# Row lengths of the Gram matrix added in PSUM, four wide comparisons, and edge sums per batch, in a hypergraph, attention and filter kernel

## What is computed

```
sq = sum(xf * xf, axis=-1)
d2 = sq[:, :, None] + sq[:, None, :] - 2.0 * einsum('bic,bjc->bij', xf, xf)
incidence = sqrt(maximum(d2, 0)) < 16.0
xe = einsum('bnc,dc->bnd', xf, W_fc) + b_fc
deg_e = sum(incidence, axis=1)
edge = einsum('bve,bvc->bec', incidence, xe) / deg_e
vert = einsum('bve,bec->bvc', incidence, edge) / deg_v
x = x + silu(batchnorm(vert + xf))
```

## Time and profile before

| | |
|---|---|
| median of 3 runs | 52.59 us |
| lowest and highest | 52.2 and 52.71 us |
| the profiled execution's own time | 52.18 us |
| its span, first to last instruction | 50.4 us |
| PE / DVE / ACT / POOL busy in it | 42.9 / 23.3 / 21.0 / 9.6 us |

### The profile page before, as it was taken

The page is one execution under the profiler, slowest core; times in us unless marked ns, Lnnn a source line. Parts: engine busy times, 40 slices in busy tenths (PEclk is TensorE's granted clock), DMA queues, the critical chain, the costliest instruction groups (busy, mean ns, idle before and its releaser), DMA issues.

```text
span 50.4 us, 1575 instructions
## 1 busy us (share of the span) xinstructions
PE 42.9 (85%) x658; PEld 25.5 (51%) x658; DVE 23.3 (46%) x81; ACT 21.0 (42%) x55; POOL 9.6 (19%) x36
## 2 busy tenths in 40 slices
PE   2999994999879999787999968648999999999910
PEld 1332743564436974436787424226455646548800
DVE  1057629999756460326648775745001400403420
ACT  0664999805222992499895882050003100000000
POOL 4760408880002275000000000430000000000000
PEclk9999999999999999999999999999999999999999
DMA  0599400000000000000000000000000000000011
GB/s 0 145 311 362 142 0 0 0 0 0 13 0 0 0 20 0 0 0 0 0 13 0 0 13 0 0 0 0 0 0 0 7 0 0 13 0 0 0 52 52
DMA packets 1303, 1.44 MB, mean 29 GB/s; under 512 B 272, under 2 KB 1040, under 8 KB 1296
## 3 DMA queue, kind: packets, MB, share of 16 engines
q1 hardware_dynamic: 1008, 1.26, 7.8%
q10 hardware_dynamic: 288, 0.08, 0.7%
HBM read 1.21 MB, written 0.13 MB: 27 GB/s over the span
## 4 chain that ended last, share of the span: by engine, by line
PE 57%; DVE 13%; ACT 9%; issue 7%; POOL 5%; DMA 4%; POOLq 0%; DVEq 0%
PE bank L536 22%; PE bank L362 8%; DMA x_sb<-in_x 4%; PE bank L579 4%; PE bank L350 3%; PE bank L370 3%; PE quad L527 3%; ACT L252 3%; PE bank L478 2%; PE quad L492 2%; PE bank L503 2%; DVE hgraph L647 2%; POOL h L202 1%; PE quad L469 1%; POOL tiny L205 1%
## 5 line engine op out<-in xcount | busy, mean ns | idle before, releaser
L536 PE MATMUL bank<-v,gh 128*128 128x512 f16 (+7 forms) x48 | 7.5, 317 | 0.0
L536 PEld LDWEIGHTS bank<-v,gh 128*128 128x128 f16 x48 | 4.2, 98 | 3.4 <-issue 0.2
L252 ACT ACT_TABLE_LOAD x4 | 5.1, 1283 | 1.7 <-PEq L852 1.6
L337 PE MATMUL bank<-busy 128*128 128x512 f16 x9 | 4.0, 629 | 0.9 <-DVE busy L613 0.9
L536 PE MATMUL bank<-v,gl 128*128 128x512 f16 (+7 forms) x24 | 3.8, 317 | 0.8 <-DVE v L775 0.8
L362 PE MATMUL bank<-phis,mst 32*32 32x64 f32 x256 | 4.2, 289 | 0.0
L788 DVE TENSOR_TENSOR yb<-bank,maskp 128x512 f32<-128x512 f32 x2 | 1.4, 690 | 5.9 <-PE bank L536 5.9
L362 PEld LDWEIGHTS bank<-phis,mst 32*32 32x32 f32 x256 | 3.7, 110 | 0.5 <-issue 0.5
L647 DVE TENSOR_SCALAR hgraph<-quad,thr 128x256 f16<-128x256 f32 x8 | 3.4, 471 | 0.4 <-PE quad L392 0.4
L337 PE MATMUL quad<-busy 128*128 128x512 f16 x10 | 3.3, 381 | 0.0
L536 PEld LDWEIGHTS bank<-v,gl 128*128 128x128 f16 x24 | 2.0, 98 | 2.4 <-issue 1.1
(11 more groups left out here) (171 smaller groups left out, 77.3 us busy)
## 6 DMA issues: line engine op xcount, KB each, us to landing
m_sb<-in_mfilt SPq DMA_DIRECT2D x1, 512.0 KB, 3.6
cst<-in_consts SPq DMA_DIRECT2D x1, 271.0 KB, 3.8
x_sb<-in_x SPq DMA_DIRECT2D x1, 128.0 KB, 2.1
phi_sb<-in_phi SPq DMA_DIRECT2D x1, 128.0 KB, 2.5
out<-res SPq DMA_DIRECT2D x2, 64.0 KB, 1.5
sml<-in_small ACTq DMA_DIRECT2D x1, 64.0 KB, 2.6
mu_sb<-in_mu SPq DMA_DIRECT2D x1, 64.0 KB, 3.5
sml<-in_small ACTq DMA_DIRECT2D x1, 12.0 KB, 2.3
```

The source lines that it names most:

```text
L252: act.activation(spare[:, len(loads) - 1:len(loads)], eps[:, 0:1], func)
L337: pe.matmul(dst, busy[:, 0:1].broadcast_to([P, P]), busy[:, 0:1].broadcast_to([P, 512]), start=True, stop=True)
L536: mm = pe.matmul(acc[:, :, lag:HT], g[:, s, :, :].rearrange("p e a -> p (e a)"), v2[:, part, :, begin + lag:begin + HT], start=(first and ...
```

## The change

The row term of the distance is now added in PSUM as well, by 16 further matmuls whose weights are `hq` and whose moving operand is -0.5 (`neghalf`, now 256 columns wide). The 4 matmuls with `maskhalf`, the tile itself with its POOL fills, and the thresholds `thr` on DVE are gone. The additions are ordered by part, all with the high part first, and PE waits for the low part only ahead of the second. With nothing left that differs from row to row, the comparison uses the constant -128 and takes a whole batch of 512 columns at once: four comparisons in place of eight. `edge_sums` waits for its batch's comparison; the two of batch 3 now stand together ahead of the matmul with `ones32`.

```diff
--- before.py
+++ after.py
@@ -79,8 +79,7 @@
         mu_sb = sb("mu_sb", [P, NX, C])
         mumix = sb("mumix", [P, NX, C])
         mtap = sb("mtap", [P, C])
-        neghalf = sb("neghalf", [P, P], F16)
-        maskhalf = sb("maskhalf", [P, B], F16)
+        neghalf = sb("neghalf", [P, T], F16)
         hq = sb("hq", [P, 2, T], F16)
         ones32 = sb("ones32", [P, P])
         busy = sb("busy", [P, 1], F16)
@@ -102,7 +101,6 @@
         st = sb("st", [P, 8])
         h = sb("h", [P, T])
         hsq = sb("hsq", [P, T])
-        thr = sb("thr", [P, 2, B])
         hb = sb("hb", [P, T])
         hgraph = sb("hgraph", [P, B, 2, T], F16)
         h2 = sb("h2", [P, 2, T], F16)
@@ -183,10 +181,6 @@
                 pool.wait_ge(sem("pool_step"), step[0])
 
             pool.memset(neghalf[:, :], -0.5).then_inc(sem("half"), 1)
-            link(pool.memset(maskhalf[:, :], 0.0))
-            for b in range(B):
-                pool.memset(maskhalf[32 * b:32 * b + 32, b:b + 1], -0.5).then_inc(sem("half"), 1)
-            pool.wait_ge(sem("half"), 1 + B)
             pool.memset(u2[:, :, 0:PAD], 0.0).then_inc(sem("zero"), 1)
             pool.memset(ones32[:, :], 1.0).then_inc(sem("ones"), 1)
             pool.iota(tpos[:, :], [[1, T]], base=0, channel_multiplier=0,
@@ -378,21 +372,24 @@
                 for n in range(2):
                     pe.matmul(quad[:, b, n * T:(n + 1) * T], h[r, n * HT:(n + 1) * HT], h[r, :],
                               start=(n == 0), stop=False, skip_group_check=True)
-            pe.wait_ge(sem("half"), 1 + B)
+
+            pe.wait_ge(sem("half"), 1)
             pe.wait_ge(sem("hsq_high"), 1)
-            pe.wait_ge(sem("hsq_low"), 1)
-            for n in range(2):
-                for part in range(2):
-                    mm = pe.matmul(gbank[0][:, n * B:(n + 1) * B], hq[:, part, n * HT:(n + 1) * HT],
-                                   maskhalf[:, :], start=(part == 0), stop=(part == 1))
-            mm.then_inc(sem("sqi_psum"), 1)
-            for b in range(B):
-                r = slice(32 * b, 32 * b + 32)
-                for part in range(2):
-                    mm = pe.matmul(quad[:, b, :], neghalf[r, :],
+            for part in range(2):
+                if part:
+                    pe.wait_ge(sem("hsq_low"), 1)
+                for n in range(2):
+                    for b in range(B):
+                        r = slice(32 * b, 32 * b + 32)
+                        pe.matmul(quad[:, b, n * T:(n + 1) * T], hq[r, part, n * HT:(n + 1) * HT], neghalf[r, :],
+                                  start=False, stop=False, skip_group_check=True)
+                for b in range(B):
+                    r = slice(32 * b, 32 * b + 32)
+                    mm = pe.matmul(quad[:, b, :], neghalf[r, 0:P],
                                    hq[r, part, :].unsqueeze(1).broadcast_to([32, 2, T]),
                                    start=False, stop=(part == 1), skip_group_check=True)
-                mm.then_inc(sem(f"gram{b}"), 1)
+                    if part:
+                        mm.then_inc(sem(f"gram{b}"), 1)
 
             pe.wait_ge(sem("ident16"), 1)
             pe.wait_ge(sem("h_high"), 1)
@@ -406,7 +403,7 @@
 
             def edge_sums(b, n):
 
-                pe.wait_ge(sem("compare"), 2 * b + n + 1)
+                pe.wait_ge(sem("compare"), b + 1)
                 acc = edgebank[0][:, :, b, :] if b < B - 1 else edgebank[1][:, :, 0, :]
                 for half in range(2):
                     pairs = hgraph[:, b, n, half * P:(half + 1) * P]
@@ -434,11 +431,11 @@
                     elif b or n:
                         fill()
             edge_sums(B - 1, 0)
+            edge_sums(B - 1, 1)
             pe.wait_ge(sem("ones"), 1)
             pe.wait_ge(sem("bp"), 1)
             pe.matmul(gbank[0][:, 2 * B:2 * B + 1], ones32[:, :], bp, start=True, stop=True)\
               .then_inc(sem("bound_psum"), 1)
-            edge_sums(B - 1, 1)
             fill()
             pe.wait_ge(sem("rdeg"), 2)
             turn_rows(gbank[1], rdeg[:, :, :].rearrange("p h b -> p (h b)"), "rdegc_psum")
@@ -637,15 +634,11 @@
             dve.wait_ge(sem("phi_in"), 16)
             dve.tensor_reduce(phimax, phi_sb[:, :], AX_X, ALU.max, apply_absolute_value=True)\
                .then_inc(sem("phimax"), 1)
-            dve.wait_ge(sem("sqi_psum"), 1)
-            dve.tensor_scalar(thr[:, :, :].rearrange("p h b -> p (h b)"), gbank[0][:, 0:2 * B], -1.0, -RADIUS2 / 2,
-                              ALU.mult, ALU.add).then_inc(sem("thr"), 1)
-
-            def compare(b, n):
+            def compare(b):
 
                 dve.wait_ge(sem(f"gram{b}"), 1)
-                dve.tensor_scalar(hgraph[:, b, n, :], quad[:, b, n * T:(n + 1) * T], thr[:, n, b:b + 1],
-                                  None, ALU.is_gt).then_inc(sem("compare"), 1)
+                dve.tensor_scalar(hgraph[:, b, :, :].rearrange("p n t -> p (n t)"), quad[:, b, :], -RADIUS2 / 2,
+                                  1.0, ALU.is_gt, ALU.mult).then_inc(sem("compare"), 1)
 
             def degrees(acc, first, last):
                 dve.wait_ge(sem("edge_psum"), last)
@@ -662,25 +655,20 @@
                 dve.tensor_tensor(edge2[:, 1, :, first:last, :], edge[:, :, first:last, :],
                                   edge2[:, 0, :, first:last, :], ALU.subtract).then_inc(sem("edge_low"), 1)
 
-            dve.wait_ge(sem("thr"), 1)
-            compare(0, 0)
-            compare(0, 1)
-            compare(1, 0)
-            compare(1, 1)
-            compare(2, 0)
+            compare(0)
+            compare(1)
+            compare(2)
             dve.wait_ge(sem("wts"), 1)
             dve.wait_ge(sem("sig"), 2)
             mark(dve.scalar_tensor_tensor(out=wsum[:, 0, :], in0=wts, scalar=sig, in1=sml[:, P_EXPERT:P_EXPERT + NX],
                                           op0=ALU.mult, op1=ALU.mult, accum_out=ws))
-            compare(2, 1)
+            compare(3)
             settle()
-            compare(3, 0)
             dve.wait_ge(sem("rowphi"), 1)
             dve.wait_ge(sem("mul1"), 1)
             dve.scalar_tensor_tensor(out=bp, in0=rowphi, scalar=ws, in1=mul1, op0=ALU.mult, op1=ALU.add)\
                .then_inc(sem("bp"), 1)
             degrees(edgebank[0], 0, B - 1)
-            compare(3, 1)
             mark(dve.tensor_scalar(wsp, ws, PTOP / 4, None, ALU.mult))
             dve.wait_ge(sem("rdeg"), 1)
             edges_scaled(edgebank[0], 0, B - 1)
```

## The result

The changed kernel takes 52.3 us (median of 22 runs, 51.79 to 52.52) against 52.64 us for the one before on the same chips (22 runs, 52.08 to 53.65): a ratio of 0.9947, 95% interval 0.9922 to 0.9972. That is 0.28 us faster, with 0.15 to 0.41 as the interval. The result lies within the 1% band of the forecast and inside its range, but the gain is four times the 0.07 us that was worked out. The profiled execution took 51.90 us with a span of 50.1.

A forecast was written before the change was run, and what follows sets the result against it. One dependent sequence was taken as the bound, through batch 3's scaled edges, with PE's queue the new limit. Gain 0.19 - s (s 0.12) = 0.07 us: profiled 52.18 to 52.11, median 52.5, range 52.1 to 52.95.

The forecast's parts named there:

- the 1% band of the forecast: Whole kernel: time within about 1% (0.53 us) of the kernel before, given a chance of 0.81.
- the 0.07 us that was worked out: Batch 3's edges: start at 11.53 + s against 11.72, a gain of 0.19 - s, or 0.07 us.
- The price of the row term on PE: PE's Gram stage: 0.28 us removed, four rounds of 0.10 added, so the turn of h comes 0.12 us later.
- The shift s = 0.12 of everything behind it: From PE's turn of h onward: turn and first comparison 0.12 us later; bounds zero and 0.52.
- PE as the new limit (11.53 + s): Batch 3's edges: PE's queue through hb and the edge sums sets their start, at 11.65; DVE waits.
- chain B: Not forecast, named after measuring: from wsum over the fourth comparison and bp into the ones32 matmul, toward batch 3's edges.
- P: Chain forecast to hold the end: PE's queue through ht, rowm, hb and the edge sums; batch 3's edges at 11.65.
- The sign that I had named for P: DVE before the first reciprocals: a new wait for the edge sums, with batch 3's edges at 11.6 to 11.7.
- The wide comparison: DVE comparisons of 512 columns: interval 0.66 us, length 0.74; all four 2.64 against 3.12 us.
- DVE's cut counts in full: Rival on DVE: the comparisons' 0.51 us come off entirely, giving 52.1 us; chance 0.12.
- Wide comparisons do gain: Denies a DVE rival: no gain per column (0.78 us each), 0.09 slower, 52.7 us; chance 0.12.
- The new matmuls run side by side: Denies a PE rival: matmuls one after another, 1.60 us instead of 0.40, total 53.7; chance 0.10.

The follow-up runs named there:

- experiment 2: Also spelled `mask`: changed kernel with four full-row matmuls put back after the Gram matrix, result unused, and maskhalf back; ratio 0.9937 to the kernel before.
- after_phis: Changed kernel with POOL's product phis moved ahead of the expert weights; median 51.94 us, ratio 0.9908 to the kernel before.
- again: Changed kernel run once more, unaltered, for a second trace; 51.99 us.
- late: Changed kernel with two useless matmuls of 448 columns ahead of the turn of h on PE; ratio 0.9956 to the kernel before, traced execution 52.59 us.
- norow: Changed kernel without the sixteen row-term matmuls, so it computes another incidence; a single execution, 52.31 us.
- narrow: Changed kernel's row term in PSUM, but eight comparisons of 256 columns and the old edge-sum order; ratio 0.9996 to the kernel before.
- best2: Changed kernel: phis early, fourth comparison before wsum, bnd after batch 3's edges, hb matmul after vertex sums, convolution's matmul before first mixing; 51.34 us, ratio 0.9805.

## Why the prediction was right, and where its sizes were off

**The price of the row term on PE** (0.12 us, dropping 0.28 for L386 and the changes of mode, adding four rounds of 0.10): right. It measured 0.12 from the last Gram round to the turn, and L386 with its changes of mode 0.32 where it was put back (experiment 2).

**The shift s = 0.12 of everything behind it**: this is the step that failed. I added it to one execution's Gram stage as if that were fixed. The stage lasts 1.17 to 2.11 us between executions of the same instructions, because the pace of its rounds changes at a moment that moves. In the execution of the earlier trace rows its four rounds start at 4.86, 5.45, 5.88 and 6.12 us, in the changed kernel's at 4.86, 5.45, 5.75 and 5.97. While the pace is slow the second distance is 0.43 us (all distances behind the first in `after_phis`); afterwards it is 0.22. The bridging matmuls ahead of it, 512 columns each, follow at 0.43 us too, against 0.22 for 512 columns in the additions. That is 1.2 and 2.4 columns per ns (512 / 0.427 and 512 / 0.216), so I take it for TensorE's two levels of 1.2 and 2.4 GHz; the records don't show the lower one, as the granted clock is 1.00 in the stretches on either side. In the profiled pair it gave the changed kernel 0.15 us, so s was -0.02.

**PE as the new limit (11.53 + s)**: right only for the executions in which PE is late enough. From the last additions to the edges of batch 3:

| run | last additions | edges of batch 3 | between |
|---|---|---|---|
| changed | 6.84 | 11.45 | 4.61 |
| `again` | 6.92 | 11.53 | 4.61 |
| `mask` | 6.81 | 11.41 | 4.60 |
| `late`, 0.38 us added behind | 6.84 | 11.83 | 4.61 + 0.38 |
| `after_phis` | 7.47 | 12.08 | 4.61 |

Forecast were 6.98 and 11.65, so 4.67. But there is a floor that I left out: `wsum` + 1.89 (chain B, which holds the 0.12 us of `bp` beside `mumix`; the prediction has `bp` start at 10.32 and gives it no more than its old length). In the changed kernel's trace and in `mask` both chains arrive together; P alone sets the end in `again`, `late` and `after_phis`. The edges start at the later of the last additions + 4.61 and `wsum` + 1.89. The kernel before is `wsum` + 2.2. With the Gram stage of the earlier trace rows the last additions would start at 6.12 + 0.87 = 6.99 and the gain would be 11.72 - 11.60 = 0.12 us, near the 0.07 forecast; where PE is earlier, it is 2.2 - 1.89 = 0.3, and I assume about the same where `wsum` is held by `phis` in both kernels. The times speak for the latter kinds: 13 of the changed kernel's 22 executions took 52.29 to 52.33 us, `norow` with its held `wsum` took 52.31, and with `phis` moved none of 12 lay there. That is argued from groups of times; only one trace shows a held `wsum`. By these groups the limit in most executions was not the PE chain of the forecast. That the time came out within 1% says little for it: the band is 0.53 us wide to either side, and a gain of 0.12 and one of 0.3 both fall inside. The sign that I had named for P, a wait of DVE for the edge sums ahead of the first reciprocals, is absent in the changed kernel's profile and present (0.30 us) in `after_phis`; the edges, at 11.45, came before the 11.6 to 11.7.

**The wide comparison** (interval 0.66, length 0.74): measured 0.60 and 0.69. I had added the new columns to the comparison with a column of thresholds; with a constant the one of 256 columns is shorter from the start (0.41 in `narrow`, not 0.47). This lowers chain B, not P.

**The rivals.** That DVE's cut counts in full did not happen (0.28 of 0.51). Wide comparisons do gain. The new matmuls run side by side, four per round of 0.11 us.

## What to carry to other kernels

When a change removes the longer of two chains that end close together, work out the floor of both, and ask which of them varies between executions; one trace gives one draw of it. An engine that idles before a wait (DVE before `wsum`) while it has ready work behind the wait shows where reordering pays: here reordering (`best2`, 2%) was worth more than the comparisons that were saved (0.5%). And an instruction that only feeds something later (`bnd`, the matmul on `hb`) should not stand ahead of one on the chain. Look also at how long the small instructions on the chain last: moved earlier, `bp` came to lie beside an instruction of POOL and lost there most of the 0.14 us it had gained.

## What the runs showed of the hardware

- A DVE instruction of four columns took 0.69 us in place of 0.22 beside a POOL instruction that began 0.06 us after it. At the same distance it took 0.22 in the other traces, so the outcome is decided below what they resolve. Only one trace shows it for `wsum`; that the upper group of times in the kernel before comes from it rests on that group's absence once `phis` was moved.
- Another DVE instruction with two SBUF inputs, `bp` (one column), took 0.26 to 0.37 us in place of 0.21 to 0.23 in six traces, each time over 0.01 us after a POOL instruction that had begun before it.
- PE's pace changed from 0.43 to 0.22 us per round at a moment between 4.0 us (`norow`, whose bridging matmul at 3.87 is followed by one at 4.11) and 6.8 us (`after_phis`, where the Gram rounds are 0.43 apart to the end, at 6.73), with the same instructions ahead of it. What sets the moment stays open.
